# Eight pairs of fields: VectorE operands moved to PSUM, shared sums taken out a chunk later, layer-0 products spread through layer 1, and a new chunk table

## What is computed

```python
e = stack([tbl_f[ids[:, f]] for f in range(39)], axis=1)      # 512 x 39 x 16
x = prev = e
for k in range(3):                                            # 128 units each
    z = einsum('bmd,bhd->bdmh', x, prev).reshape(b, D, m * h) # products of fields and units
    t = einsum('bdc,co->bdo', z, ws[k]) + bs[k]
    t = transpose(t, (0, 2, 1))
    t = t / sqrt(sum(t * t, axis=(-2, -1)))                   # one norm per sample
    logit.append(t); prev = t
z = sum(concatenate(logit, axis=1), axis=-1)                  # 512 x 384
h = relu(concatenate([z, dense_ctx], 1) @ W_top1 + b_top1)    # 400 -> 512
h = relu(h @ W_top2 + b_top2)                                 # 512 -> 256
y = h @ W_top3
```

## Time and profile before

| | |
|---|---|
| median of 3 runs | 1233.92 us (1232.56 to 1234.36) |
| the profiled execution | 1234.13 us |
| its span | 1232.3 us |
| PE busy | 1156.4 us, 94% |
| DVE busy | 965.7 us, 78% |
| POOL busy | 649.9 us, 53% |
| ACT busy | 113.7 us, 9% |
| mean granted clock of PE | 0.993 |

### The profile page before, as it was taken

One profiled execution on the slowest core, in us unless ns is written; L12 is line 12 of the kernel. 1 busy time (PEld: TensorE's weight loads), 2 busy tenths in 40 slices (PEclk: granted clock), 3 DMA queues, 4 the chain that ended last, 5 costly groups with the idle time before them and its releaser, 6 DMA issues. The chain is left out here.

```text
span 1232.3 us, 19609 instructions
## 1 busy us (share of the span) xinstructions
PE 1156.4 (94%) x7100; PEld 513.7 (42%) x7100; DVE 965.7 (78%) x836; ACT 113.7 (9%) x219; POOL 649.9 (53%) x486
## 2 busy tenths in 40 slices
PE   0889999999999999999999999999999999999899
PEld 0334443444444344444444444444444443444443
DVE  1677878887887988788888878888887888888772
ACT  0010010100001010000101000010101001010102
POOL 5446655555665555566455556545556654533440
PEclk9899999999999999999999999999999999999989
DMA  6948275452826536283653628355362835537010
GB/s 164 393 147 295 66 245 154 145 194 82 306 71 233 164 135 204 65 305 89 224 163 130 219 62 304 93 212 167 112 245 62 285 112 197 172 112 250 1 45 1
DMA packets 97751, 204.14 MB, mean 166 GB/s; under 512 B 46571, under 2 KB 49515, under 8 KB 93638
## 3 DMA queue, kind: packets, MB, share of 16 engines
q1 hardware_dynamic: 90954, 202.38, 49.0%
q0 software_dynamic: 5120, 1.29, 1.0%
q10 hardware_dynamic: 1660, 0.25, 0.2%
HBM read 201.70 MB, written 2.16 MB: 165 GB/s over the span
## 5 line engine op out<-in xcount | busy, mean ns | idle before, releaser
L553 DVE TENSOR_TENSOR z<-t_ps,xb 128x2048 f32<-128x2048 f32 (+1 forms) x352 | 706.7, 2042 | 190.0 <-PE acc L700 133.1
L686 PE MATMUL acc<-z,w_sb 128*64 128x512 f32 x2944 | 650.2, 596 | 7.4 <-DVE z L553 7.4
L288 POOL TENSOR_TENSOR sums<-z 128x512 f32<-128x512 f32 x128 | 163.0, 1273 | 459.0 <-DVE z L553 459.0
L686 PEld LDWEIGHTS acc<-z,w_sb 128*64 128x64 f32 x2944 | 213.0, 138 | 403.2 <-issue 384.6
L291 POOL TENSOR_TENSOR sums<-z,sums 128x1024 f32<-128x1024 f32 x128 | 303.0, 2367 | 10.0
L700 PE MATMUL mix_ps<-sums,s_sb 128*64 128x256 f32 x1024 | 194.2, 382 | 29.8 <-POOL sums L291 29.7
L253 POOL DMA_INDIRECT gathered<-in_table,rows_of x160 | 171.8, 1074 | 67.9 <-issue 52.9
L700 PE MATMUL acc<-z,w_sb 128*64 128x256 f32 x512 | 152.8, 380 | 4.3 <-DVE z L553 4.3
L700 PE MATMUL mix_ps<-z,w_sb 128*64 128x256 f32 x512 | 152.8, 380 | 0.0
L700 PE MATMUL p_ps<-z,w_sb 128*64 128x256 f32 x512 | 152.8, 380 | 0.0
L700 PE MATMUL acc<-z,s_sb 128*64 128x256 f32 x512 | 152.8, 380 | 0.0
(11 more groups left out here) (73 smaller groups left out, 374.9 us busy)
## 6 DMA issues: line engine op xcount, KB each, us to landing
xb<-xt SPq DMA_DIRECT2D x80, 768.0 KB, 4.8
xb<-xq SPq DMA_DIRECT2D x64, 512.0 KB, 4.4
xb<-xt SPq DMA_DIRECT2D x64, 512.0 KB, 5.7
xb<-xt SPq DMA_DIRECT2D x32, 1024.0 KB, 5.5
xr<-xt SPq DMA_DIRECT2D x144, 156.0 KB
x<-xt SPq DMA_DIRECT2D x45, 78.0 KB
gathered<-in_table,rows_of POOLq DMA_INDIRECT x160
xr<-xt SPq DMA_DIRECT2D x32, 78.0 KB
```

The source lines that it names most:

```text
L288: nc.gpsimd.tensor_tensor(t2, t3, b11, ALU.add).then_inc(sums_ready, 1)
L553: nc.vector.tensor_tensor(z[:, at:at + n, :], t_ps[k - 1][:, :].rearrange("p (a n) -> p a n", a=1).broadcast_to([P, n, N]), xb[:, XB_ROW[c ...
L686: last = nc.tensor.matmul(acc[k][o, :], w_sb[k][:, field + r, o], z[:, at + r, :], start=(c == 0 and r == 0), stop=(c == NCH - 1 and r == ...
```

## The change

It has six parts.

1. The order of chunk sizes: `PLAIN_IN` goes from 3, 3, P, P, 4, 3, P, P, 4, 3, 3 to 4, 3, P, P, 3, 3, P, P, 4, 3, 3. The ring is still 14 slots. The positions are now written out, and the distances `RING_BACK` follow: for layer 1 from 4, 4, 4, 4, 3, 3, 3, 3, 2, 3, 7 to 4, 4, 4, 3, 3, 3, 4, 4, 3, 3, 4, and the same again for layer 2.
2. The shared sums and `add_shared` of the layer before stand one chunk later (behind c2 and c3), the norm sums behind c5.
3. The four parts of `products0` stand behind c6, c7, c9 and c10 of layer 1 instead of all behind c10, and read their first operand from `t_ps[1]`, into which ACT copies `x3` (`copy_x`).
4. The operands of the shared sums, the norm's small tensors and `scale0` lie in PSUM where DVE read two from SBUF before; ACT's one copy of 64 x 512 becomes two of 64 x 256.
5. `norm_sums` does the plain sum before the sum of squares, and both of them behind c3 of layer 2.
6. In layer 2, `normalize` and `scale0` stand behind c10 instead of c9.

```diff
-PLAIN_IN = [3, 3, 0, 0, 4, 3, 0, 0, 4, 3, 3]
+PLAIN_IN = [4, 3, 0, 0, 3, 3, 0, 0, 4, 3, 3]
...
+RING_AT = [0, 4, 7, 0, 4, 7, 10, 0, 4, 8, 11, 0, 4, 7, 0, 4, 7, 10, 0, 4, 8, 11]
...
+        nrm, root, prod, half, dsum = (
+            nrm_ps[:, r * LAYERS * TILE_B:(r + 1) * LAYERS * TILE_B].rearrange("p (k b) -> p k b", k=LAYERS)
+            for r in range(5))
...
+            def copy_x(i):
+
+                act.wait_ge(x3_loaded, 16 * PER_STEP * (i + 1))
+                act.wait_ge(z_ready, STEPS * (i - 1))
+                nc.scalar.copy(t_ps[1][0:WIDE, :], x3[:, :]).then_inc(x3_copied, 1)
...
-                nc.scalar.copy(cross[RIGHT, :], mix_ps[LEFT, :]).then_inc(cross_ready, 1)
+                nc.scalar.copy(cross[RIGHT, N2], mix_ps[LEFT, N2]).then_inc(cross_ready, 1)
+                nc.scalar.copy(p7_ps[RIGHT, N2], mix_ps[LEFT, N1]).then_inc(cross_ready, 1)
...
+                if not last:
+                    copy_x(i + 1)
                 carry(i, 1)
...
-                dve.wait_ge(x3_loaded, 16 * PER_STEP * (i + 1))
+                if at_first(i):
+                    dve.wait_ge(x3_loaded, 16 * PER_STEP)
+                    x = x3[:, :]
+                else:
+                    dve.wait_ge(x3_copied, i)
+                    x = t_ps[1][0:WIDE, :]
...
-                nc.vector.tensor_tensor(v[RIGHT, N2], v[RIGHT, N1], cross[RIGHT, N1], ALU.add).then_inc(v_step, 1)
+                nc.vector.tensor_tensor(v[RIGHT, N2], v[RIGHT, N1], p7_ps[RIGHT, N2], ALU.add).then_inc(v_step, 1)
...
-                nc.vector.tensor_tensor(by_sample(t_ps[0][:, :]), by_sample(traw0[:, :]),
-                                        over_d(rnorm[:, 0, :]), ALU.mult).then_inc(t0_ready, 1)
+                nc.vector.scalar_tensor_tensor(by_sample(t_ps[0][:, :]), by_sample(acc0[:, :]), bias[:, 0:1],
+                                               over_d(rnorm[:, 0, :]), ALU.add, ALU.mult).then_inc(t0_ready, 1)
...
                     products(i, 1, c)
-                    if c == 1 and not first:
+                    if c == 2 and not first:
                         shared_sums(i - 1, 2)
-                    if c == 2 and not first:
+                    if c == 3 and not first:
                         add_shared(i - 1, 2)
-                    if c == 4 and not first:
+                    if c == 5 and not first:
                         norm_sums(2, i - 1)
                     if c == 6 and first:
                         mixed_weights(2)
-                if not last:
-                    products0(i + 1, (0, 1))
+                    if c in (6, 7, 9, 10) and not last:
+                        products0(i + 1, ((6, 7, 9, 10).index(c),))
                 shared_sums(i, 1)
-                if not last:
-                    products0(i + 1, (2, 3))
                 add_shared(i, 1)
                 for c in range(NCH):
                     products(i, 2, c)
                     if c == 3:
                         norm_sums(1, i)
-                    if c == 4 and not last:
+                    if c == 3 and not last:
                         norm_sums(0, i + 1)
-                    if c == 9:
+                    if c == 10:
                         normalize(i + 1, *layers_of(first, last))
```

More of the change, by code:

```diff
@@ L75, with ring_back @@
 RING = 14
[L78 to L98, removed]
+RING_AT = [0, 4, 7, 0, 4, 7, 10, 0, 4, 8, 11, 0, 4, 7, 0, 4, 7, 10, 0, 4, 8, 11]
+def ring_back(s):
+    n = CHUNKS[s % NCH][2]
+    for d in range(1, STEPS + 1):
+        r = (s - d) % STEPS
+        if RING_AT[r] < RING_AT[s] + n and RING_AT[s] < RING_AT[r] + CHUNKS[r % NCH][2]:
+            return d
+RING_BACK = [ring_back(s) for s in range(STEPS)]
 SUM_SLOTS = 2
@@ L149, in build @@
         cross = sb("cross", [P, N])
-        u2 = sb("u2", [P, H])
         ssum = sb("ssum", [P, LAYERS, TILE_B])
-        dsum = sb("dsum", [P, LAYERS, TILE_B])
-        root = sb("root", [P, LAYERS, TILE_B])
         inv = sb("inv", [P, LAYERS, TILE_B])
-        prod = sb("prod", [P, LAYERS, TILE_B])
-        half = sb("half", [P, LAYERS, TILE_B])
         rnorm = sb("rnorm", [P, LAYERS, TILE_B])
@@ L182, in build @@
         nrm_ps = pb("nrm_ps")
-        nrm = nrm_ps[:, 0:LAYERS * TILE_B].rearrange("p (k b) -> p k b", k=LAYERS)
+        nrm, root, prod, half, dsum = (
+            nrm_ps[:, r * LAYERS * TILE_B:(r + 1) * LAYERS * TILE_B].rearrange("p (k b) -> p k b", k=LAYERS)
+            for r in range(5))
         h1_ps = [acc0, acc[1], mix_ps, p7_ps]
@@ L196, in build @@
         ones_ready, pads_ready = sem("ones_ready"), sem("pads_ready")
-        x3_loaded = sem("x3_loaded")
+        x3_loaded, x3_copied = sem("x3_loaded"), sem("x3_copied")
         xr_loaded = [sem(f"xr_loaded{g}") for g in range(len(LOADS0))]
@@ L451, in carry, with evacuate1 @@
                     act.wait_ge(v_used, n)
-                nc.scalar.copy(cross[RIGHT, :], mix_ps[LEFT, :]).then_inc(cross_ready, 1)
+                nc.scalar.copy(cross[RIGHT, N2], mix_ps[LEFT, N2]).then_inc(cross_ready, 1)
+                nc.scalar.copy(p7_ps[RIGHT, N2], mix_ps[LEFT, N1]).then_inc(cross_ready, 1)
                 act.wait_ge(v_step, 5 * n + 2)
-                nc.scalar.copy(cross[LEFT, N1], u2[RIGHT, :]).then_inc(u2_ready, 1)
+                nc.scalar.copy(cross[LEFT, N1], cross[RIGHT, N2]).then_inc(u2_ready, 1)
                 nc.scalar.copy(v[LEFT, N1], mix_ps[RIGHT, N1]).then_inc(p1_ready, 1)
-            def evacuate1(i):
+            def evacuate1(i, last=False):
                 act.wait_ge(v_used, mix_no(i, 1) + 1)
+                if not last:
+                    act.wait_ge(z0_ready, len(LOADS0) * (i + 2))
                 nc.scalar.copy(t_ps[1][:, :], raw12[:, :]).then_inc(t1_ready, 1)
@@ L478, in tile @@
                     evacuate2(i - 1)
+                if not last:
+                    copy_x(i + 1)
                 carry(i, 1)
-                evacuate1(i)
+                evacuate1(i, last)
                 if not last:
@@ L537, in products0 @@
                         xr[0:n, k0:k1, :],
-                        x3[0:n, :].rearrange("p (a n) -> p a n", a=1).broadcast_to([n, k1 - k0, N]),
+                        x[0:n, :].rearrange("p (a n) -> p a n", a=1).broadcast_to([n, k1 - k0, N]),
                         xr[0:n, k0:k1, :], ALU.mult).then_inc(z0_ready, 1)
@@ L560, in shared_sums @@
                 n = mix_no(i, k)
-                dve.wait_ge(cross_ready, n + 1)
-                nc.vector.tensor_tensor(u2[RIGHT, :], cross[RIGHT, N2], mix_ps[RIGHT, N1], ALU.add).then_inc(v_step, 1)
+                dve.wait_ge(cross_ready, 2 * n + 1)
+                nc.vector.tensor_tensor(cross[RIGHT, N2], cross[RIGHT, N2], mix_ps[RIGHT, N1],
+                                        ALU.add).then_inc(v_step, 1)
                 dve.wait_ge(v_step, 5 * n + 1)
-                nc.vector.tensor_tensor(u2[RIGHT, :], u2[RIGHT, :], mix_ps[RIGHT, N2], ALU.add).then_inc(v_step, 1)
+                nc.vector.tensor_tensor(cross[RIGHT, N2], cross[RIGHT, N2], mix_ps[RIGHT, N2],
+                                        ALU.add).then_inc(v_step, 1)
                 dve.wait_ge(v_step, 5 * n + 2)
-                nc.vector.tensor_tensor(v[RIGHT, N1], u2[RIGHT, :], p7_ps[RIGHT, N1], ALU.add).then_inc(v_step, 1)
+                dve.wait_ge(cross_ready, 2 * n + 2)
+                nc.vector.tensor_tensor(v[RIGHT, N1], cross[RIGHT, N2], p7_ps[RIGHT, N1], ALU.add).then_inc(v_step, 1)
                 dve.wait_ge(v_step, 5 * n + 3)
-                nc.vector.tensor_tensor(v[RIGHT, N2], v[RIGHT, N1], cross[RIGHT, N1], ALU.add).then_inc(v_step, 1)
+                nc.vector.tensor_tensor(v[RIGHT, N2], v[RIGHT, N1], p7_ps[RIGHT, N2], ALU.add).then_inc(v_step, 1)
                 dve.wait_ge(u2_ready, n + 1)
@@ L589, in norm_sums @@
                 dve.wait_ge(sq_ready[k], i + 1)
-                nc.vector.tensor_reduce(ssum[:, k, :], by_sample(sq[:, min(k, 1), :]),
-                                        axis=AX_X, op=ALU.add).then_inc(ssum_ready[k], 1)
                 if k != 1:
@@ L594, in norm_sums @@
                 nc.vector.tensor_reduce(dsum[:, k, :], by_sample(raw[:, :]), axis=AX_X, op=ALU.add)
+                nc.vector.tensor_reduce(ssum[:, k, :], by_sample(sq[:, min(k, 1), :]),
+                                        axis=AX_X, op=ALU.add).then_inc(ssum_ready[k], 1)
             def normalize(event, k0, k1):
@@ L671, in layer0 @@
                     pe.wait_ge(raw_ready[0], i)
+                    pe.wait_ge(t0_ready, i)
                 for g, (k0, k1) in enumerate(LOADS0):
```

## The result

The changed kernel takes 1203.99 us (median of 4 runs, 1203.37 to 1204.45) against 1233.31 (4 runs beside it, 1232.56 to 1234.36): a ratio of 0.9761, 95% interval 0.9744 to 0.9778. 1202.3 was forecast. The profiled execution took 1204.42 with a span of 1202.6.

The account below looks back on a forecast made before the run. PE was taken as the bound, waiting in the loop only for POOL's second sum. 1234.13 - 37.3 (loop) + 5.0 (tile 0) + 0.5 (end) = 1202.3 us; range 1197 to 1214, some 8 in 10.

Parts of the forecast that it names:

- The loop: Tiles 1 to 15: both of PE's waits for POOL's second sum go, together -37.3 us.
- the two waits: PE waiting for POOL's second sum in c2 and c3 of layer 1: 1.13 + 1.41 = 2.54 us a tile.
- The products of c2: DVE's products for c2 of layer 1: ready 5.25 us before PE starts c2, where 3.1 is needed.
- POOL's start on them: POOL's sums for c2 of layer 1 were to start 5.15 us before PE's c2.
- c6's start: DVE's products for c6 of layer 1 were to start 6.1 us after PE starts c2.
- the room at c6: Layer 1's thinnest margin: c6's products ready at 8.4 us after PE's c2 starts, needed at 8.8, so 0.4 us.
- The PSUM operands by themselves I cost at nothing: DVE instructions reading PSUM instead of SBUF: no time added to the sum.
- Rival 5: POOL's c6 sums and DVE's `products0` collide at SBUF ports: 8 to 22 us; chance 0.17 together with another rival.
- Tile 0: DVE waits for tile 1's rows ahead of c7, shifting everything behind: +5.0 us, bounds 3.8 to 9.
- half-us sums of traffic: Estimate from DMA traffic that the first part of tile 1's rows lands 5.2 us after SP issues the load.
- The end: Start of layer 2 in the last tile: c0 is one field more, +0.5 us.
- the 1.7 that I took: Tile 15, without mixed rows: the same c2 and c3 waits cost about 1.7 us, 1.2 of it idle.

Follow-up runs that it names:

- the table alone: The kernel before with only the new order of chunk sizes and the ring distances that follow from it: 1197.0 us, ratio 0.9708.
- the order alone: The kernel before with only the new order of DVE's instructions, old chunk sizes and ring, operands in SBUF: 1207.86 us, ratio 0.9794.
- one reduction and three: The changed kernel with one or three unused reductions added on DVE ahead of c6 of layer 1: 1205.38 us with one, 1222.73 with three.

## Why the prediction was right

**The loop: right.** The step from the two waits to 2.54 us a tile measured 72.35 - 69.84 = 2.51 (560.87 to 633.22 before, 563.39 to 633.23 after, POOL's starts on c2 and c6). The products of c2 were forecast ready 5.25 us ahead of PE, and were 5.1 (613.51 + 6.15 against 624.77); POOL's start on them was counted at 5.15 ahead and was 4.9, with the 0.24 us wait behind `scale0` left out. c6's start came out at 6.1 as counted. That the margins are real is shown from both sides: 3.1 us of lead is enough (the table alone), 2.5 is not (the order alone), and the room at c6 is 0.4 us (one reduction and three).

**What the parts are worth.** I forecast the six parts together, and two of them do the same thing. The table alone gives the loop's whole gain, the order alone all but 0.8 us a tile, and both no more than the table. The changed kernel with tile 0 as before (1196.64) is as fast as these two parts without the others (1196.99), so the remaining parts are worth nothing that can be measured. "The PSUM operands by themselves I cost at nothing" holds for their durations: `products0` takes 1213 ns on average against 1215 before, so the 65 ns more that the Trainium skill's page "VectorE: DVE Perf Modes", section on the TRN2 errata, would give for a PSUM source are not in this trace. Rival 5 put a price of 8 to 22 us on two SBUF operands in the new place; it is 20. So the copy of `x3` pays only for moving `products0` next to POOL's sums, and moving it there gains nothing in the loop and costs 5.6 to 8.5 us in tile 0.

**Tile 0: the mechanism right, the size 5.0 instead of 7.3** (the bounds were 3.8 to 9). Three things make the difference in this execution. The weights and SP's issue of `x` came 0.5 us later than in the kernel before (66.61 and 68.06 against 66.11 and 67.54). The first part of the rows was there 74.08 - 68.06 = 6.0 us after the issue, where half-us sums of traffic gave 5.2 (the sum used 72.6, which is 5.1); in the three other runs with the part ahead of c7 it was 5.5 to 6.0. Why it is longer is not shown; the sums assume that transfers end in the order of issue. And c7 itself ran 5.81 us instead of 4.95: the granted clock over it was 0.51 of full speed on average, where it was 0.66 before. The sum had no term for that. PE's wait ahead of c7 was 7.4 us and not the 9 forecast, since PE came to c7 3.3 us later than before, which the wait swallowed.

**The end: +0.5 forecast and measured, and 1.2 us of luck.** The wait ahead of c0 grew from 3.36 to 3.90 as forecast. What shrank is the stretch at the lower clock behind it: 28 rows, 6.0 us at full clock, in 7.92 us, against 24, 5.14 at full clock, in 8.30. In the loop and tile 15 together, 35.8 + 0.5 = 36.3 were saved instead of 37.3. Tile 15 gave the 1.7 that I took (before, c2 and c3 took 4.04 and 3.68 us there, 1140.11 to 1147.83). What is missing is in the loop: I took one inner tile for all 14, but the two waits cost 2.51 in tiles 2 to 13, 2.12 in tile 1 and 2.41 in tile 14, 34.7 together instead of 35.6. By the three stretches the forecast was +5.0, -37.3 + 0.5 = -36.8 and 0; measured were +7.3, -35.8 and -1.2. The misses of +2.3, +1.0 and -1.2 are the 2.1 us between 1202.3 and the profiled 1204.42. So a part of the closeness is luck: the clock at the end gave back what the loop fell short by.

## What to carry to other kernels

When the engine that bounds the time waits on a chain through two others, work out how far ahead the first of them must be and what each edit does to that one number; two edits that raise it past the need are worth one, and the smallest is enough. Before spreading work into an earlier gap, ask for its inputs in the first iteration as well, where the queues hold them back. Moving an operand to PSUM paid in this kernel only where the instruction ran beside GpSimd's sums, and there it was worth 20 us. And look at the distance between starts as well as at the list of waits and the total: 0.2 us a tile stood in neither of them.

## What the runs showed of the hardware

- In the run with `x3` read from SBUF, a DVE instruction with two SBUF operands and a POOL sum exclude each other, and the record of the one that waits gets longer rather than later: POOL's L278 2.19 and 2.27 us instead of 1.28, DVE's product 2.55 instead of 1.21. A short one (0.42 us) started just ahead of a POOL sum of 2.37 lengthens it by 0.16 only (in the two runs with the new order and SBUF operands).
- After the wait of 3.4 to 3.9 us in the last tile PE runs for a time at the lower of its two clock levels (1.2 GHz of 2.4), and how long differs from run to run: the mean granted clock over the rows of c0 and c1 was 0.78 in the changed kernel, 0.63 in the kernel before and 0.70 with `x3` in SBUF. 28 rows of c0 and c1, 6.0 us at full clock, took 7.67 to 7.93 us in seven kernels and 8.85 in an eighth, and 24 rows, 5.14 at full clock, took 8.30 in the kernel before and 7.07 in the one with the order alone. So one such wait costs 1.7 to 3.2 us beyond itself, and a difference of 1 us between two executions need not come from their code.
